# GpSimd adds the whole adjacency mask, TensorE adds none of it, and VectorE makes the mask at the end of its step

## The chip, the cores and the metric
The kernel runs on one core of one Trainium2 chip. The metric is the time of one execution on the device, in microseconds (us), given as the median of several runs. The core has five engines that run their own instruction streams and wait for each other by semaphores: TensorE (PE in the rows; PEld is its weight load), VectorE (DVE), ScalarE (ACT), GpSimd (POOL) and SyncE (SP, which here only issues DMAs). A semaphore wait holds back everything that stands behind it on its engine.

## The reference
One graph attention layer on 4096 nodes, all inputs float32 except the 4096 x 4096 integer adjacency `adj`:

```
h        = relu(layernorm(x))                                   # 4096 x 256
neib_att = tanh(neigh @ Wn1 + bn1) @ Wn2 + bn2                   # 4096 x 32
value    = neigh @ Wv + bv                                       # 4096 x 128
x_att    = tanh(h @ Wx1 + bx1) @ Wx2 + bx2                       # 4096 x 32
ws       = leaky_relu(x_att @ neib_att.T, slope 0.01)            # 4096 x 4096
ws       = where(adj > 0, ws, -9e15); ws = softmax(ws, axis=1)
out      = x + concat([h @ Wfx + bfx, ws @ value], axis=1)       # 4096 x 256
```

## The kernel before
A first phase (to about 47 us) makes `neib_att` and turns `neigh` for `value`. The main phase goes over the 4096 x 4096 scores in **chunks** of 128 rows by 1024 columns, two PSUM banks each: 4 chunks make a tile of 128 rows, 4 tiles a group, 8 groups the matrix, 128 chunks in all. `main` gives every engine the same step counter s, and in step s each engine does its part of several chunks. The order on each engine is written out by hand in its `step` function; nothing else schedules. For chunk s:

- VectorE makes the mask (`mask_of`, L642): 0 where there is an edge, -2^53 where there is none, bf16, 128x1024, from the loaded adjacency. Two mask buffers take turns, four `adj_in` slots are filled two at a time.
- TensorE makes the scores (`score`, L860 and L861) in two halves of 512 columns, in one of two PSUM buffers. Up to chunk 18 (`POOL_MASKS` = 19) an identity matmul L860 first adds the mask to both halves. From chunk 19 on it does so for the first half only.
- ScalarE writes 99 x relu(score) to SBUF (the "rise", L512).
- GpSimd adds the mask to the second half in SBUF (L421), from chunk 19 on.
- VectorE joins PSUM and SBUF into the leaky scores with a running row maximum (the "reduce", L676; a custom instruction over 1024 columns). This is in step s + 1, and its end (`leaked`) gives the PSUM buffer free for the scores of chunk s + 2.
- ScalarE does the exponentials two chunks at a time (L524, 2048 columns), five steps later, so in every odd step.

Nineteen steps behind, the second half of the pipeline turns the exponentials of a whole group (L884, four 128x128 transposes for each of 32 column blocks), splits the result in a high part (`hi`, ScalarE L489) and a low part (`lo`, VectorE L655), and multiplies both with the values (L903, L904, L905). Each step does two blocks, called u = 0 and u = 1. In the steps that are left of a group of 16, the next group's rows are normalised, turned and multiplied (VectorE L546 to L611, GpSimd's Newton steps L375 to L392 and sums L357 and L364), and finished rows are written.

VectorE's order in a step from 19 on is: reduce of chunk s-1, `lo` 0, mask of chunk s+1, `lo` 1, and the small work of the group. TensorE's is: turn 0, scores, product of the last step's block 0, turn 1, product of the last step's block 1, small work. GpSimd's is: add of chunk s, in odd steps the DMA of two adjacency chunks (L400), sums, Newton steps.

Of the kernel before, what the change touches and what calls it, by code (L numbers as in the profile page):

```python
# [27 lines left out]
BF16 = mybir.dt.bfloat16  # L28
INT32 = mybir.dt.int32
ALU = mybir.AluOpType  # L30
# [3 lines left out]
P = 128  # L34
N_X, N_NEIGH, D_IN, D_HID, D_OUT = 4096, 4096, 256, 32, 128
KT = D_IN // P
BANK = 512
GROUP = BANK
TILES = GROUP // P
GROUPS = N_X // GROUP  # L40
NEIGH_GROUPS = N_NEIGH // GROUP
CHUNK = 2 * BANK
CHUNKS = N_NEIGH // CHUNK
STEPS = GROUPS * TILES * CHUNKS
GSTEPS = TILES * CHUNKS
BLOCKS = N_NEIGH // P
PERIOD = 2 * GSTEPS
# [31 lines left out]
X_LEFT_LOAD, X_SUM = 4, 9  # L79
X_RIGHT = 6  # L80
V_START, V_STRIDE = 1, 2
POOL_MASKS = BACK_LAG
WARM_UP = 12
NEWTON = 3
NEWTON_OPS = 2 + 4 * NEWTON
# [2 lines left out]
def build(nc, x, adj, neigh, wx1, bx1, wx2, bx2, wn1, bn1, wn2, bn2, wv, bv, wfx, bfx, out):  # L88
    with ExitStack() as ctx:
        def sb(name, shape, dt):  # L90
            return ctx.enter_context(nc.sbuf_tensor(name, shape, dt))
# [20 lines left out]
        b_fx = sb("b_fx", [P, 1, D_OUT], FP32)  # L112
        ident = sb("ident", [P, P], FP32)
        b_v = sb("b_v", [P, 1, D_OUT], FP32)
        ident_bf16 = sb("ident_bf16", [P, P], BF16)
        top = sb("top", [P, 2, CHUNKS], FP32)
        neg_top = sb("neg_top", [P, 2, 1], FP32)
        sums = sb("sums", [P, 2, TILES, HALVES], FP32)
# [224 lines left out]
        @block.gpsimd  # L343
        def _(pool):
            pool.memset(ident[:, :], 0.0).then_inc(fills, 1)
            pool.memset(ident_bf16[:, :], 0.0).then_inc(fills, 1)
            pool.wait_ge(fills, 2)
            pool.affine_select(out=ident[:, :], in_=ident[:, :], compare_op=ALU.not_equal, fill=1.0,
                               base=0, pattern=[[-1, P]], channel_multiplier=1).then_inc(made, 1)
            pool.affine_select(out=ident_bf16[:, :], in_=ident_bf16[:, :], compare_op=ALU.not_equal, fill=1.0,  # L350
                               base=0, pattern=[[-1, P]], channel_multiplier=1).then_inc(made, 1)

            def left_sum(e, h):
# [59 lines left out]
                right_sum(0, h)  # L413

            def step(s, it):
                if POOL_MASKS <= s < STEPS:

                    parity, tile, c = chunk_of(s)
                    pool.wait_ge(risen, s + 1 + PERIOD * it)
                    half = scores[:, parity * TILES + tile, c * CHUNK + BANK:(c + 1) * CHUNK]  # L420
                    pool.tensor_tensor(half, half, mask[:, s % 2, BANK:CHUNK], ALU.add).then_inc(masked, 1)  # L421
                n = s - LOAD + 1 + ADJ_RING
                if n % LOAD == 0 and ADJ_RING <= n < STEPS:
                    pool.wait_ge(mask_done, s + 1 + PERIOD * it)
                    load_adj(n, n // CHUNKS + 2 * TILES * it)
                for i in range(2):
                    if e := x_due(s, X_SUM + i):
                        left_sum(e + 2 * it, i)
                for i in range(2):
                    if (g := right_due(s - i)) is not None:  # L430
                        right_sum(g + 2 * it, i)
                for i in range(NEWTON + 1):
                    if e := x_due(s, X_RSTD[i]):
                        rstd_of(e + 2 * it, i)
# [104 lines left out]
        def _(dve):  # L539
# [94 lines left out]
            def mask_of(n, it):  # L634

                k = n + PERIOD * it
                dve.wait_ge(adj_ready[n % ADJ_RING // LOAD], 16 * (n // ADJ_RING + 1) + 16 * PERIOD // ADJ_RING * it)
                if n >= 2:
                    dve.wait_ge(scored, k - 1)
                if n - 2 >= POOL_MASKS:  # L640
                    dve.wait_ge(masked, k - 1 - POOL_MASKS)
                dve.tensor_scalar(mask[:, n % 2, :], adj_in[:, n % ADJ_RING, :], 0.0, MASKED, ALU.is_le,  # L642
                                  ALU.mult).then_inc(mask_done, 1)

# [11 lines left out]
                                  ALU.subtract).then_inc(lo_done, 1)  # L656

            def step(s, it):
                if s < POOL_MASKS:
                    mask_of(s + 1, it)  # L660
                n = s - 1
                if 0 <= n < STEPS:

                    parity, tile, c = chunk_of(n)
                    k = n + PERIOD * it
                    cols = scores[:, parity * TILES + tile, c * CHUNK:(c + 1) * CHUNK]
                    dve.wait_ge(risen, k + 1)
                    if n >= POOL_MASKS:
                        dve.wait_ge(masked, k + 1 - POOL_MASKS)
                    if c:  # L670
                        dve.wait_ge(leaked, k)
                    start = top[:, tile % 2, c - 1:c] if c else -3.0e38
                    if c == 0 and n >= 2 * CHUNKS:
                        dve.wait_ge(top_done, n // CHUNKS - 1 + 2 * TILES * it)
                    dve.sem_inc(joined, 1)
                    dve.tensor_tensor_reduce(cols, ps[:, n % 2], cols, SLOPE, start, ALU.add, ALU.max,  # L676
                                             top[:, tile % 2, c:c + 1]).then_inc(leaked, 1)
                lo(s, 0, it)
                if POOL_MASKS <= s < STEPS - 1:
                    mask_of(s + 1, it)  # L680
                if value_due(s - 2) is not None:
                    value_low(value_due(s - 2))
                if s == 1:
                    att_high(1, NEIGH_GROUPS - 1)
                    att_low(1, NEIGH_GROUPS - 1)
                lo(s, 1, it)
                if 0 <= n < STEPS and n % CHUNKS == CHUNKS - 1:
                    dve.wait_ge(leaked, n + 1 + PERIOD * it)
                    if n >= 2 * CHUNKS:

                        dve.wait_ge(exp_done, (n // CHUNKS - 1) * HALVES + 2 * TILES * HALVES * it)
                    dve.tensor_scalar(neg_top[:, n // CHUNKS % 2, :], top[:, n // CHUNKS % 2, CHUNKS - 1:CHUNKS],
                                      -1.0, None, ALU.mult).then_inc(top_done, 1)
# [46 lines left out]
        def _(pe):  # L740
# [91 lines left out]
                if i == TILES - 1:  # L832
                    last.then_inc(x_wide, 1)

            pe.wait_ge(made, 2)
            for _ in range(WARM_UP):
                pe.transpose(pa[:, 1, 0:P], ident[:, :], ident[:, :])
            turn_rows(0, 0, 0)
# [3 lines left out]
            def score(s, h, it):  # L842

                if s >= STEPS:
                    return
                k = s + PERIOD * it
                parity, tile, c = chunk_of(s)
                if h == 0:
                    pe.wait_ge(mask_done, k + 1)
                    if s >= 2:  # L850
                        pe.wait_ge(leaked, k - 1)
                    if s < CHUNKS:

                        pe.wait_ge(att_out, NEIGH_GROUPS - 1 if s == 1 else (s + 1) * CHUNK // GROUP)
                    if tile == 0 and c == 0:
                        pe.wait_ge(x_att, s // GSTEPS + 2 * it + 1)
                half = slice(h * BANK, (h + 1) * BANK)
                on_pool = h == 1 and s >= POOL_MASKS
                if not on_pool:
                    pe.matmul(ps[:, s % 2, half], ident_bf16[:, :], mask[:, s % 2, half], start=True, stop=False)  # L860
                last = pe.matmul(ps[:, s % 2, half], xs[:, parity, tile * P:(tile + 1) * P],  # L861
                                 neib[:, c * CHUNK + h * BANK:c * CHUNK + (h + 1) * BANK], start=on_pool, stop=True)
                if h == 1:
                    last.then_inc(scored, 1)

# [98 lines left out]
```

## Time and profile before

| what | value |
|---|---|
| time, median of 3 runs | 548.64 us (547.9 to 549.05) |
| the profiled execution | 552.71 us, span 550.5 us |
| TensorE busy | 505.3 us, 92% |
| VectorE busy | 478.2 us, 87% |
| ScalarE busy | 432.7 us, 79% |
| GpSimd busy | 211.8 us, 38% |
| mean granted TensorE clock | 0.983 of full speed |

The span is the time from the first to the last instruction of the profiled execution. Busy time is time in which an engine's compute instructions run; the ends of matmuls are modelled and overlap, so the distance from one matmul's start to the next says more than its length. A group of 16 steps repeats itself in the middle of the run with a period of 59.0 us.

### The profile page before, as it was taken

Reading aid. Unit: us, or ns where it says so; the run is one execution under the profiler, and the core shown is the slowest. Engines: PE = TensorE matmul, PEld = TensorE weight load, DVE = VectorE, ACT = ScalarE, POOL = GpSimd, SP = SyncE. Lnnn points to the kernel's source line nnn. Section 1 sums busy time; section 2 is a strip of 40 time slices with the busy share of each in tenths; the row PEclk is TensorE's granted clock in tenths of the full one; section 3 lists DMA queues with packets and bytes.
Section 4 is the critical chain, followed back from the end, with each engine's and each line's share of the span. In section 5 each row is a group of like instructions: output and inputs, shape, how many; then the busy total and the mean of one; then the engine's idle time right before and its main releaser. Section 6 shows DMA issues by size and latency. Waiting matters only on the chain.

```text
span 550.5 us, 8742 instructions
## 1 busy us (share of the span) xinstructions
PE 505.3 (92%) x2759; PEld 378.3 (69%) x2759; DVE 478.2 (87%) x883; ACT 432.7 (79%) x585; POOL 211.8 (38%) x325
## 2 busy tenths in 40 slices
PE   5798788899999999999999999999999999998996
PEld 4455556677777767766877677766777686776784
DVE  2669897999999999999999999999998999996664
ACT  2563688898888888888888878888888889897553
POOL 1402123234633654355434553456435444440100
PEclk8898999899999999999999999999999999999999
DMA  7752865454456545664356445643565445620100
GB/s 205 190 166 48 143 135 98 92 115 78 76 87 139 89 69 96 117 135 76 59 107 147 73 78 113 119 91 64 95 114 96 77 74 94 113 46 1 40 1 19
DMA packets 38013, 52.00 MB, mean 94 GB/s; under 512 B 3920, under 2 KB 29776, under 8 KB 37968
## 3 DMA queue, kind: packets, MB, share of 16 engines
q0 software_dynamic: 9216, 33.56, 37.5%
q1 hardware_dynamic: 28752, 17.90, 11.3%
q8 instruction: 22, 0.36, 0.3%
q14 instruction: 23, 0.19, 0.1%
HBM read 80.81 MB, written 4.19 MB: 154 GB/s over the span
## 4 chain that ended last, share of the span: by engine, by line
PE 34%; DVE 16%; issue 11%; ACT 11%; POOL 7%; DMA 3%; DVEq 1%; POOLq 0%; ACTq 0%
PE ps_turned L884 10%; POOL scores L421 6%; DVE pt_lo L655 5%; PE ps_scores L861 5%; PE ps_product L903 4%; PE ps_product L905 4%; PE ps_product L904 4%; ACT scores L512 4%; ACT scores L524 4%; DVE mask L642 4%; DVE scores L676 3%; PE ps_scores L860 3%; DMA adj_in<-in_adj 3%; ACT pt_hi L489 2%; PE ps_product L814 1%
## 5 line engine op out<-in xcount | busy, mean ns | idle before, releaser
L421 POOL TENSOR_TENSOR scores<-scores,mask 128x512 f32<-128x512 f32 x109 | 129.2, 1186 | 203.6 <-ACT scores L512 203.6
L655 DVE TENSOR_TENSOR pt_lo<-ps_turned,pt_hi 128x512 fp32r<-128x512 f32 x256 | 175.1, 685 | 32.1 <-ACT pt_hi L489 15.9
L489 ACT ACTIVATE pt_hi<-ps_turned 128x512 fp32r<-128x512 f32 x256 | 152.5, 597 | 55.6 <-PE ps_turned L884 49.5
L884 PE MATMUL ps_turned<-ident,scores 128*128 128x128 f32 x1024 | 158.3, 277 | 11.4 <-DVE pt_lo L655 11.0
L884 PEld LDWEIGHTS ps_turned<-ident,scores 128*128 128x128 f32 x1024 | 119.9, 141 | 61.3 <-DVE pt_lo L655 30.4
L512 ACT ACTIVATE scores<-ps_scores 128x1024 f32<-128x1024 f32 x128 | 131.1, 1025 | 28.7 <-PE ps_scores L861 25.9
L524 ACT ACTIVATE scores<-scores,neg_top 128x2048 f32<-128x2048 f32 x64 | 127.9, 1998 | 0.0
L676 DVE CUSTOM_DVE_ANT_0 scores<-ps_scores,scores,top 128x1024 f32<-128x1024 f32 x96 | 122.2, 1273 | 2.8 <-ACT scores L512 0.9
L903 PE MATMUL ps_product<-pt_hi,v_hi 128*128 128x512 f32 x256 | 113.1, 442 | 0.2 <-DVE pt_lo L655 0.2
L861 PE MATMUL ps_scores<-neib,xs 128*128 128x512 f32 x256 | 109.9, 507 | 0.0
L905 PE MATMUL ps_product<-pt_lo,v_hi 128*128 128x512 f32 x256 | 101.4, 396 | 0.0
L904 PE MATMUL ps_product<-pt_hi,v_lo 128*128 128x512 f32 x256 | 100.6, 393 | 0.0
L642 DVE TENSOR_SCALAR mask<-adj_in 128x1024 bf16<-128x1024 bf16 x128 | 87.8, 687 | 5.7 <-DMA adj_in<-in_adj 5.5
L860 PE MATMUL ps_scores<-mask,ident_bf 128*128 128x512 bf16 x147 | 57.2, 389 | 16.5 <-DVE mask L642 10.4
L905 PEld LDWEIGHTS ps_product<-pt_lo,v_hi 128*128 128x128 f32 x256 | 48.0, 188 | 11.1
L861 PEld LDWEIGHTS ps_scores<-neib,xs 128*128 128x128 f32 x256 | 49.9, 195 | 3.8
L903 PEld LDWEIGHTS ps_product<-pt_hi,v_hi 128*128 128x128 f32 x256 | 48.4, 189 | 5.4 <-DVE pt_lo L655 0.7
L904 PEld LDWEIGHTS ps_product<-pt_hi,v_lo 128*128 128x128 f32 x256 | 48.7, 190 | 4.6
L400 POOL DMA_DIRECT2D adj_in<-in_adj x64 | 36.9, 577 | 32.5 <-DVE mask L642 32.4
L676 DVE CUSTOM_DVE_ANT_0 scores<-ps_scores,scores 128x1024 f32<-128x1024 f32 x32 | 39.0, 1219 | 4.5 <-issue 2.0
L860 PEld LDWEIGHTS ps_scores<-mask,ident_bf 128*128 128x128 bf16 x147 | 14.3, 97 | 31.5 <-DVE mask L642 18.9
L830 PEld LDWEIGHTS ps_product<-w_fx,x_rows_t 128*128 128x128 f32 x128 | 19.8, 199 | 2.6
(76 smaller groups left out, 385.1 us busy)
## 6 DMA issues: line engine op xcount, KB each, us to landing
adj_in<-in_adj POOLq DMA_DIRECT2D x64, 512.0 KB, 5.5
scores<-in_L_gnn_neigh SPq DMA_DIRECT2D x8, 512.0 KB, 4.3
x_rows<-in_x SPq DMA_DIRECT2D x8, 512.0 KB, 6.6
x_left<-in_x SPq DMA_DIRECT2D x8, 256.0 KB, 5.7
x_right<-in_x SPq DMA_DIRECT2D x8, 256.0 KB, 2.9
out_h<-x_left SPq DMA_DIRECT2D x8, 256.0 KB, 2.3
out_h<-x_right SPq DMA_DIRECT2D x8, 256.0 KB, 5.1
scores<-in_x SPq DMA_DIRECT2D x1, 512.0 KB, 5.0
```

The source lines that it names most:

```text
L421: pool.tensor_tensor(half, half, mask[:, s % 2, BANK:CHUNK], ALU.add).then_inc(masked, 1)
L489: act.activation(pt_hi[:, (2 * b + u) % HI_RING], pt[:, u], ACT.Copy).then_inc(hi_done, 1)
L512: act.activation(scores[:, parity * TILES + tile, c * CHUNK:(c + 1) * CHUNK], ps[:, s % 2], ACT.Relu, scale=RISE).then_inc(risen, 1)
L524: act.activation(cols, cols, ACT.Exp, bias=neg_top[:, tile % 2, :], accum_out=sums[:, parity, tile, c // 2:c // 2 + 1]).then_inc(exp_done, 1)
L642: dve.tensor_scalar(mask[:, n % 2, :], adj_in[:, n % ADJ_RING, :], 0.0, MASKED, ALU.is_le, ALU.mult).then_inc(mask_done, 1)
L655: dve.tensor_tensor(pt_lo[:, u], pt[:, u], pt_hi[:, (2 * b + u) % HI_RING].bitcast(FP32), ALU.subtract).then_inc(lo_done, 1)
L676: dve.tensor_tensor_reduce(cols, ps[:, n % 2], cols, SLOPE, start, ALU.add, ALU.max, top[:, tile % 2, c:c + 1]).then_inc(leaked, 1)
L861: last = pe.matmul(ps[:, s % 2, half], xs[:, parity, tile * P:(tile + 1) * P], neib[:, c * CHUNK + h * BANK:c * CHUNK + (h + 1) * BANK], s ...
L884: last = pe.transpose(pt[:, u, i * P:(i + 1) * P], scores[:, parity * TILES + i, n * P:(n + 1) * P], ident[:, :])
L903: pe.matmul(acc, v_hi[:, n, :], pt_hi[:, b2_ % HI_RING, :], start=n == 0, stop=False)
L904: pe.matmul(acc, v_lo[:, n, :], pt_hi[:, b2_ % HI_RING, :], start=False, stop=False)
L905: pe.matmul(acc, v_hi[:, n, :], pt_lo[:, b2_ % 2, :], start=False, stop=n == BLOCKS - 1).then_inc(block_used, 1)
```

## The change
GpSimd now adds the mask of every chunk, both halves, in two instructions of 128x512, in every step from 0 on; before each pair it waits for the rise and for the mask. TensorE's identity matmuls and the bf16 identity are gone, and `score` no longer waits for the mask. In VectorE's step the mask of the next chunk is made after `lo` 1 in all steps; before, it was made between the two `lo` from step 19 on, and ahead of the reduce in the steps up to 18. The reduce waits for both halves' adds (`masked`, now two per chunk) instead of the rise.

```
-POOL_MASKS = BACK_LAG
...
 def step(s, it):                      # GpSimd
-    if POOL_MASKS <= s < STEPS:
+    if s < STEPS:
         parity, tile, c = chunk_of(s)
-        pool.wait_ge(risen, s + 1 + PERIOD * it)
-        half = scores[:, parity * TILES + tile, c * CHUNK + BANK:(c + 1) * CHUNK]
-        pool.tensor_tensor(half, half, mask[:, s % 2, BANK:CHUNK], ALU.add).then_inc(masked, 1)
+        pool.wait_ge(risen, s + 1)
+        pool.wait_ge(mask_done, s + 1)
+        for h in range(2):
+            half = scores[:, parity * TILES + tile, c * CHUNK + h * BANK:c * CHUNK + (h + 1) * BANK]
+            pool.tensor_tensor(half, half, mask[:, s % 2, h * BANK:(h + 1) * BANK], ALU.add).then_inc(
+                masked, 1)
...
 def mask_of(n, it):                   # VectorE
     if n >= 2:
-        dve.wait_ge(scored, k - 1)
-    if n - 2 >= POOL_MASKS:
-        dve.wait_ge(masked, k - 1 - POOL_MASKS)
+        dve.wait_ge(masked, 2 * (k - 1))
...
 def step(s, it):                      # VectorE
-    if s < POOL_MASKS:
-        mask_of(s + 1, it)
...
-        dve.wait_ge(risen, k + 1)
-        if n >= POOL_MASKS:
-            dve.wait_ge(masked, k + 1 - POOL_MASKS)
+        dve.wait_ge(masked, 2 * (k + 1))
...
     lo(s, 0, it)
-    if POOL_MASKS <= s < STEPS - 1:
-        mask_of(s + 1, it)
...
     lo(s, 1, it)
+    if s < STEPS - 1:
+        mask_of(s + 1, it)
...
 def score(s, h, it):                  # TensorE
     if h == 0:
-        pe.wait_ge(mask_done, k + 1)
...
-    on_pool = h == 1 and s >= POOL_MASKS
-    if not on_pool:
-        pe.matmul(ps[:, s % 2, half], ident_bf16[:, :], mask[:, s % 2, half], start=True, stop=False)
     last = pe.matmul(ps[:, s % 2, half], xs[:, parity, tile * P:(tile + 1) * P],
-                     neib[:, ...], start=on_pool, stop=True)
+                     neib[:, ...], start=True, stop=True)
```

GpSimd, steps 76 to 78 (the middle of the main phase): before, two steps stand merged in the first row, then the DMA, six Newton steps and the next add.

```order
184 L421 TENSOR_TENSOR scores<-scores,mask 128x512 [waits risen] x2
185 L400 DMA adj_in<-in_adj 128x2048 [waits mask_done]
186 L375 TENSOR_SCALAR var_eps<-mean_var 128x4 [waits newton,aggr_done,x_normed]
187 L379 TENSOR_SCALAR rstd<-var_eps 128x4 [waits newton]
188 L385 TENSOR_TENSOR factor<-rstd 128x4 [waits newton]
189 L387 TENSOR_TENSOR factor<-factor,var_eps 128x4 [waits newton]
190 L390 TENSOR_SCALAR factor<-factor 128x4 [waits newton]
191 L392 TENSOR_TENSOR rstd<-rstd,factor 128x4 [waits newton]
192 L421 TENSOR_TENSOR scores<-scores,mask 128x512 [waits risen]
```

The same place of the changed kernel:

```order
304 L418 TENSOR_TENSOR scores<-scores,mask 128x512 [waits mask_done,risen]
305 L418 TENSOR_TENSOR scores<-scores,mask 128x512
306 L418 TENSOR_TENSOR scores<-scores,mask 128x512 [waits mask_done,risen]
307 L418 TENSOR_TENSOR scores<-scores,mask 128x512
308 L395 DMA adj_in<-in_adj 128x2048 [waits mask_done]
309 L370 TENSOR_SCALAR var_eps<-mean_var 128x4 [waits newton,aggr_done,x_normed]
...
314 L387 TENSOR_TENSOR rstd<-rstd,factor 128x4 [waits newton]
315 L418 TENSOR_TENSOR scores<-scores,mask 128x512 [waits mask_done,risen]
316 L418 TENSOR_TENSOR scores<-scores,mask 128x512
```

Each step has two adds back to back, and the DMA and the Newton steps stand behind both.

VectorE, step 77, from the reduce of chunk 76 to that of chunk 77, before:

```order
486 L676 ISA scores,top<-ps_scores,scores 128x1024 [waits top_done,risen,masked]
487 L676 ISA top 128x1
488 L655 TENSOR_TENSOR pt_lo<-ps_turned,pt_hi 128x512 [waits block_used,hi_done]
489 L642 TENSOR_SCALAR mask<-adj_in 128x1024 [waits masked,scored,adj_ready1]
490 L655 TENSOR_TENSOR pt_lo<-ps_turned,pt_hi 128x512 [waits block_used,hi_done]
491 L554 BN_AGGR mean_var<-stats 128x2 [waits newton,stats_done,x_normed]
492 L554 BN_AGGR mean_var<-stats 128x2 x3
493 L600 TENSOR_SCALAR xs<-ps_product,b 128x512 [waits scored,x_second]
494 L676 ISA scores,top<-ps_scores,scores,top 128x1024 [waits leaked,risen,masked]
```

And in the changed kernel:

```order
428 L668 ISA scores,top<-ps_scores,scores 128x1024 [waits masked,top_done]
429 L668 ISA top 128x1
430 L651 TENSOR_TENSOR pt_lo<-ps_turned,pt_hi 128x512 [waits block_used,hi_done] x2
431 L638 TENSOR_SCALAR mask<-adj_in 128x1024 [waits masked,adj_ready1]
432 L552 BN_AGGR mean_var<-stats 128x2 [waits newton,stats_done,x_normed]
433 L552 BN_AGGR mean_var<-stats 128x2 x3
434 L598 TENSOR_SCALAR xs<-ps_product,b 128x512 [waits scored,x_second]
435 L668 ISA scores,top<-ps_scores,scores,top 128x1024 [waits masked,leaked]
```

The mask now stands behind both `lo` and ahead of the group's small work, which stands between it and the next reduce.

## Rows read from the trace of the kernel before

**Rows 1.** Busy time in stretches of 18, 107 and 16 steps, each from one reduce's start.

```profile
core 0: us, PE busy (x) PEld busy (x) DVE busy (x) ACT busy (x) POOL busy (x), PEclk, DMA share, GB/s
51.21:100.57 49.36, 41.30 (x248) 29.83 (x246) 42.56 (x87) 37.27 (x43) 9.85 (x25) 0.97 0.66 118
104.52:494.90 390.38, 373.17 (x2059) 282.66 (x2057) 370.07 (x680) 338.28 (x455) 186.03 (x253) 1.00 0.52 95
273.49:332.51 59.02, 56.53 (x313) 42.81 (x313) 56.33 (x107) 50.74 (x70) 29.11 (x42) 1.00 0.53 99
```

**Rows 2.** Page, groups of instructions: busy us, mean ns, idle before and releaser.

```profile
L421 POOL TENSOR_TENSOR scores<-scores,mask 128x512 f32<-128x512 f32 x109 | 129.2, 1186 | 203.6 <-ACT scores L512 203.6
...
L642 DVE TENSOR_SCALAR mask<-adj_in 128x1024 bf16<-128x1024 bf16 x128 | 87.8, 687 | 5.7 <-DMA adj_in<-in_adj 5.5
L860 PE MATMUL ps_scores<-mask,ident_bf 128*128 128x512 bf16 x147 | 57.2, 389 | 16.5 <-DVE mask L642 10.4
...
L400 POOL DMA_DIRECT2D adj_in<-in_adj x64 | 36.9, 577 | 32.5 <-DVE mask L642 32.4
```

**Rows 3.** VectorE's masks in one period, 273.49 to 332.51 us.

```profile
L642 DVE TENSOR_SCALAR mask<-adj_in 128x1024 bf16<-128x1024 bf16 x16 | 11.7, 729 | 0.3 <-DMA adj_in<-in_adj 0.3
```

**Rows 4.** Timeline, steps 76 to 79: start, us, engine, line.

```profile
311.81 0.42 DVE L642 TENSOR_SCALAR mask<-adj_in 128x1024 bf16<-128x1024 bf16 x1
...
312.41 0.66 PE L884 MATMUL ps_turned<-ident,scores 128*128 128x128 f32 x4
...
312.90 0.38 PE L860 MATMUL ps_scores<-mask,ident_bf 128*128 128x512 bf16 x1
...
313.57 0.39 PE L903 MATMUL ps_product<-pt_hi,v_hi 128*128 128x512 f32 x1
...
314.91 0.60 ACT L489 ACTIVATE pt_hi<-ps_turned 128x512 fp32r<-128x512 f32 x1
...
315.40 1.99 ACT L524 ACTIVATE scores<-scores,neg_top 128x2048 f32<-128x2048 f32 x1
...
317.76 1.27 DVE L676 CUSTOM_DVE_ANT_0 scores<-ps_scores,scores,top 128x1024 f32<-128x1024 f32 x1
...
317.86 1.02 ACT L512 ACTIVATE scores<-ps_scores 128x1024 f32<-128x1024 f32 x1
...
318.96 0.68 DVE L655 TENSOR_TENSOR pt_lo<-ps_turned,pt_hi 128x512 fp32r<-128x512 f32 x1
...
322.07 1.28 DVE L676 CUSTOM_DVE_ANT_0 scores<-ps_scores,scores,top 128x1024 f32<-128x1024 f32 x1
```

**Rows 5.** Timeline, a mask and GpSimd's two instructions around it.

```profile
245.04 1.16 POOL L421 TENSOR_TENSOR scores<-scores,mask 128x512 f32<-128x512 f32 x1 [1.65 <-ACT scores L512]
...
245.22 1.26 DVE L642 TENSOR_SCALAR mask<-adj_in 128x1024 bf16<-128x1024 bf16 x1
...
246.16 0.91 POOL L357 TENSOR_TENSOR x_left<-x_left,b_fx 128x256 f32<-128x256 f32 x1
```

**Rows 6.** Timeline, an add and the reduce that waits for it.

```profile
493.56 1.16 POOL L421 TENSOR_TENSOR scores<-scores,mask 128x512 f32<-128x512 f32 x1 [2.92 <-ACT scores L512]
...
494.90 1.28 DVE L676 CUSTOM_DVE_ANT_0 scores<-ps_scores,scores,top 128x1024 f32<-128x1024 f32 x1 [0.20 <-POOL scores L421]
```

**Rows 7.** Timeline, steps 2 to 5 and GpSimd's Newton steps of steps 13 to 15.

```profile
56.40 1.27 DVE L676 CUSTOM_DVE_ANT_0 scores<-ps_scores,scores,top 128x1024 f32<-128x1024 f32 x1
...
60.73 1.27 DVE L676 CUSTOM_DVE_ANT_0 scores<-ps_scores,scores,top 128x1024 f32<-128x1024 f32 x1
...
62.16 0.38 PE L860 MATMUL ps_scores<-mask,ident_bf 128*128 128x512 bf16 x1 [0.62 <-DVE top L676]
...
86.62 0.22 POOL L375 TENSOR_SCALAR var_eps<-mean_var 128x4 f32<-128x4 f32 x1 [4.84 <-DVE mean_var L554]
...
91.80 0.38 POOL L392 TENSOR_TENSOR rstd<-rstd,factor 128x4 f32<-128x4 f32 x1
```

More of the change, by code:

```diff
@@ L114, in build @@
         b_v = sb("b_v", [P, 1, D_OUT], FP32)
-        ident_bf16 = sb("ident_bf16", [P, P], BF16)
         top = sb("top", [P, 2, CHUNKS], FP32)
@@ L345, in _ @@
             pool.memset(ident[:, :], 0.0).then_inc(fills, 1)
-            pool.memset(ident_bf16[:, :], 0.0).then_inc(fills, 1)
-            pool.wait_ge(fills, 2)
+            pool.wait_ge(fills, 1)
             pool.affine_select(out=ident[:, :], in_=ident[:, :], compare_op=ALU.not_equal, fill=1.0,
-                               base=0, pattern=[[-1, P]], channel_multiplier=1).then_inc(made, 1)
-            pool.affine_select(out=ident_bf16[:, :], in_=ident_bf16[:, :], compare_op=ALU.not_equal, fill=1.0,
                                base=0, pattern=[[-1, P]], channel_multiplier=1).then_inc(made, 1)
@@ L833, in x_wide_layer @@
                     last.then_inc(x_wide, 1)
-            pe.wait_ge(made, 2)
+            pe.wait_ge(made, 1)
             for _ in range(WARM_UP):
@@ L857, in score @@
                 half = slice(h * BANK, (h + 1) * BANK)
-                on_pool = h == 1 and s >= POOL_MASKS
-                if not on_pool:
-                    pe.matmul(ps[:, s % 2, half], ident_bf16[:, :], mask[:, s % 2, half], start=True, stop=False)
                 last = pe.matmul(ps[:, s % 2, half], xs[:, parity, tile * P:(tile + 1) * P],
-                                 neib[:, c * CHUNK + h * BANK:c * CHUNK + (h + 1) * BANK], start=on_pool, stop=True)
+                                 neib[:, c * CHUNK + h * BANK:c * CHUNK + (h + 1) * BANK], start=True, stop=True)
                 if h == 1:
```

## Prediction, made before the changed kernel ran
> **What bounds the kernel now.** I read the windows of the main phase first, then the groups of the page, then the timeline of a few steps. The windows [rows 1] are cut at starts of the reduce L676: 18 steps take 49.36 us at the start (2.74 a step), the next 107 take 390.38 us (3.65 a step), and one period of 16 takes 59.02 us (3.69 a step). In that period VectorE is busy 56.33 us and TensorE 56.53; the reader is to see two engines near full, ScalarE 8 us below, and GpSimd at half. Part of VectorE's busy time is a stall: a mask takes 0.42 us when GpSimd is idle [rows 4], but 0.69 on average [rows 2] and 0.73 in the period [rows 3]. In [rows 5] a mask started at 245.22 while GpSimd's add ran to 246.20; the mask ended at 246.48, so it stood until the add was over and then did its work in 0.28 us. GpSimd's next instruction had begun at 246.16 and was itself held until the mask was through. So such a mask pays for the rest of the running add, and gets in between two GpSimd instructions.
> The Trainium skill, "SBUF — State Buffer", section "SBUF: two separate sides", says that VectorE in its two-port modes and GpSimd share a port pair as an exclusive lock, and that the loser blocks fully. The trace agrees (0.42 against 1.26 us), and the rule speaks against a change that doubles GpSimd's adds. It does not say who is next after two adds back to back; [rows 5] does, once.
>
> **The change part by part.**
> TensorE loses the identity matmuls, 147 of them [rows 2]. The price of one is not its modelled 389 ns but what it holds up the order: from L860 to L903 three matmuls take 0.67 us [rows 4], so 0.22 each. Scores are also no longer kept waiting by the mask (page: 16.5 us idle before L860, 10.4 by the mask). If TensorE alone set the pace that would be 147 x 0.22 = 32 us; with the wait to the mask some more.
> GpSimd gets 147 more adds. One is 1.16 to 1.19 us [rows 2, 6]; a pair 2.31, since the second begins 0.05 before the first ends, as in [rows 5]. The skill's "GPSIMD Engine Reference", section 3.1, gives 4497 ns for such an add of 2048 elements, a quarter of which is 1.12 us; the row is used. With half a DMA issue a step (0.58 / 2 [rows 2]) and 0.28 for a mask that gets in, GpSimd needs 2.9 us a step, under 3.65 but over 2.74.
> The move of the mask on VectorE adds no instruction. But the reduce waits for both adds, and the group's small work now stands behind the mask.
>
> First the middle (steps 19 to 126). Let R(n) be the start of the reduce of chunk n.
> VectorE's own work a step, each instruction counted to the start of the next: reduce 1.20, two `lo` 0.60 each, mask 0.34 unstalled: 2.74 [rows 4]. Small work: 56.33 busy less 16 x 1.20, 32 x 0.60 and 11.7 - 16 x 0.08 of masks leaves 7.5 us a period, 0.47 a step [rows 1, 3]. Together 3.2 a step: VectorE could run at 51 us a period if nothing kept it.
> Chain A: reduce n (1.20), `lo` 0 (0.68), turn 0 of the next step (0.49 to the scores), both score matmuls until ScalarE can start (0.62), rise (1.02), the pair of adds (2.31), reduce n+2. That is 6.32 us and five handoffs of 0.05 to 0.18 ([rows 6]: add's end 494.72, reduce 494.90), 0.35 together: 6.67 for two steps.
> Chain B, over the exponentials in odd steps: from the turn at 312.41 over `hi` 1 and the exponential (314.91, 315.40) to the end of the next rise at 318.88 are 6.47 us [rows 4], without the identity matmul 6.25. Before it stand reduce and `lo` of an odd chunk (1.94 with the handoff), behind it the pair and two handoffs (2.56). So R(odd n) to R(n+3) is at least 10.75.
> With w the interval to an odd chunk's reduce and y that to an even one's: w + y >= 6.67, w + 2y >= 10.75, and w >= 2.74 + 0.47 = 3.2. To each pair comes 0.1 to 0.28 for the mask that gets in or follows; with 0.2, y = (10.95 - 3.2) / 2 = 3.88, and w + y = 7.08, or 56.6 us a period against 59.02. So far the change gains: before, one such interval was 4.31 [rows 4].
> Two things eat this. First, GpSimd's other work now stands behind a pair. The Newton steps ran from 86.62 to 92.2 in three steps, and the sums are four of 0.75 (0.91 in [rows 5], held). The next pair can be ready 0.9 to 1.3 us after the reduce; 1.8 us of Newton work, or 1.1 and a DMA issue of 0.58, or two sums, comes too late. I get delays of 0.9, 0.2, 0.7 and 0.3, about 2 us a period. Second, when a mask is asked for in the second half of the pair it ends 0.28 after the pair, and the small work (0.3 to 1.0 us) then stands bare ahead of the reduce; in the present order much of it runs beside the add. The mask is asked for 2.4 us after the reduce; I laid out the 16 steps of a period with these prices, and this happens in seven of them, 0.3 to 0.65 us each less what has slack, about 2 us. The intervals came out as 3.4, 4.0, 3.45, 4.2, 3.35, 3.7, 3.1, 4.8, 3.1, 4.0, 3.8, 4.2, 3.75, 4.0, 3.55 and 4.2, together 60.6 us: 1.6 more than before. Over 107 steps, 6.7 periods, +11; the last periods have less small work, so I take +9.
>
> Then the start (steps 0 to 18), where GpSimd did no add. Here chain C closes over the two PSUM buffers: reduce n to scores of n+2 is 1.43 (60.73 to 62.16 [rows 7]), scores 0.66, rise 1.02, pair 2.31, two handoffs 0.25: 5.67 for two steps, with the mask between the halves 5.95, or 2.98 a step. GpSimd's own 2.9 is close under it, so its Newton steps (4.3 us of work in the 5.6 of [rows 7]) and sums (1.4) are paid in part; I take 3 of the 5.7. The reduce of chunk 0 waits 1.5 longer, and that of chunk 1, before at 56.40 [rows 7], comes at 57.9; 17 steps of 2.98 and 3 more end at 111.6, against 100.57. Some of this may be given back, since before, a mask waited there for its DMA (5.5 us in all [rows 2]) and that wait is now covered: +9 at the start. The adjacency load is issued after the pair now, with 5.5 us to landing; the mask that needs it comes some 7 us later, so it is hidden, by little.
> The last 50 us have no scores and no mask: nothing.
> Sum: the profiled execution is 552.71, its span 550.5 and 2.2 around it; plus 18 is 570.7. The median of the runs is 548.64, 4.1 below the profiled one, so I forecast 566.6, rounded to 566.
>
> **The bounds of what no row shows.** Two adds back to back, with a mask asking in between: at best a pair is 2.31 and the mask waits for nothing (GpSimd's side then 0.2 a step cheaper: -25), at worst each pair and mask are 2.31 + 0.42 + handoff with the small work bare each time (0.47 x 125 = 59, of which what hides under ScalarE's chain B is at least two thirds: +20 at most). I stand nearer to [rows 5], which is the same meeting once: the price of 0.28. The first scores start earlier by the mask's 0.4 us or by nothing; nothing taken.
>
> **The rivals.**
> (1) Faster: the mask's stall goes. In the period masks cost 11.7 us, 16 x 0.42 would be 6.7; if the mask always falls where VectorE would wait anyway, and TensorE gives back 0.22 a step, the middle takes the 56.6 us period of the bare chains: -2.4 x 6.7 = -16. With a start that costs only +6 (chain C without meetings, 2.84 a step, and GpSimd's other work hidden) the time is 539. For it: VectorE and TensorE are the two full engines [rows 1] and both lose work. Against: chain C is 0.1 over the present pace even at its best. It decides where GpSimd's Newton steps and sums do not reach the next pair.
> (2) No change: gain in the middle (-9) and loss at the start (+9) cancel; 549.
> (3) Much slower: GpSimd's pair is not parted, and the mask waits for the second half whenever it comes during the pair. Then about seven further steps of each period show their small work bare, at 0.26 net each: 7 x 0.26 x 6.7 = 12 more, 578. The skill's words in the section named, that the loser waits for the whole instruction, leave this open. Against it is [rows 5].
> (4) TensorE's clock: in the start it is granted 0.97 [rows 1] with TensorE busy 41.30 of 49.36 us; with the identity matmuls gone and longer waits it could fall in part of the start. At half the clock for 20 us, where it is busy half the time and the chain holds 1.1 us of it in 5.95, that is +4, 570; within my own case's range.
>
> **How the numbers follow.** My case (560 to 573): 0.60. Rival 3 and beyond: 0.17. Rival 1: 0.11. Between it and my case lies 549 to 560 with rival 2: 0.12. What a measurement can tell from no change is about 0.2%, 1.1 us. Faster 0.13, same 0.03, slower 0.84. The range from 552 to 580 leaves out rivals 1 and 2 and the far end of 3.
>
> **What would show it.** In the profile after: GpSimd busy near 384 us (211.8 of the page and 147 x 1.17); the pair 2.31, or 2.6 with a mask in it; 18 steps of the start near 58 us; a period near 60.6; VectorE's busy share lower with idle time before the reduce, released by GpSimd's add; TensorE idle before its turn, released by `lo`. A period under 58 would show that the queue behind the pair does not matter; masks with durations over 1.5 us would show rival 3. A start under 52 us would break chain C.

## The result and the profile after

| what | before | after |
|---|---|---|
| time, median | 548.85 us | 573.98 us (571.1 to 575.11, 4 runs) |
| ratio of the runs | 1 | 1.0435, 95% interval 1.0369 to 1.0501 |
| profiled execution, its span | 552.71, 550.5 | 574.46, 572.3 |
| GpSimd busy | 211.8 us | 380.3 us |
| TensorE, VectorE, ScalarE busy | 505.3, 478.2, 432.7 | 485.1, 477.3, 432.9 |

The change costs 25 us by the medians, 24 by the ratio, 21.8 between the two profiled spans; forecast were 17 to 18. The windows of the changed kernel, cut at starts of the reduce (now L668) of the same chunks as in [rows 1]: start (reduce 0 to 18), middle (19 to 126), one period (64 to 80). Columns as in [rows 1].

```profile
core 0: us, PE busy (x) PEld busy (x) DVE busy (x) ACT busy (x) POOL busy (x), PEclk, DMA share, GB/s
52.08:115.25 63.17, 42.85 (x218) 32.60 (x217) 51.73 (x88) 39.59 (x46) 51.37 (x62) 0.89 0.51 92
118.72:516.85 398.13, 353.90 (x1962) 268.20 (x1961) 360.05 (x680) 337.69 (x454) 309.66 (x361) 1.00 0.50 93
288.07:348.59 60.52, 53.38 (x298) 40.33 (x297) 54.47 (x105) 50.74 (x69) 47.24 (x58) 1.00 0.51 96
```

The start takes 13.8 us longer for 18 steps, the middle 7.8 for 107. So two thirds of the loss lie in a tenth of the run. The reader is to see that no engine is as near to full as before: in the period TensorE fell from 56.5 to 53.4 us (96% to 88%) and VectorE from 56.3 to 54.5 (95% to 90%), while the period grew by 1.5.

Groups of the page of the changed kernel, to be held against [rows 2]:

```profile
L418 POOL TENSOR_TENSOR scores<-scores,mask 128x512 f32<-128x512 f32 x256 | 299.5, 1190 | 96.8 <-ACT scores L510 96.4
...
L872 PE MATMUL ps_turned<-ident,scores 128*128 128x128 f32 x1024 | 160.2, 279 | 49.4 <-DVE pt_lo L651 48.1
...
L638 DVE TENSOR_SCALAR mask<-adj_in 128x1024 bf16<-128x1024 bf16 x128 | 87.4, 683 | 3.5 <-DMA adj_in<-in_adj 3.3
L668 DVE CUSTOM_DVE_ANT_0 scores<-ps_scores,scores 128x1024 f32<-128x1024 f32 x32 | 39.1, 1222 | 26.7 <-POOL scores L418 26.7
```

An add costs what it cost (1190 against 1186 ns), there are 147 more. The reduce, which the page of before showed waiting hardly at all for GpSimd, waits for it; for the 32 chunks at the head of a tile these are 26.7 us, for the 96 others 11.1. And TensorE idles 49.4 us ahead of its turns, 48.1 of them for VectorE's `lo`, which stands behind that reduce. This is the chain A of the prediction.

The timeline of the changed kernel over steps 76 to 78, the place of [rows 4]:

```profile
330.67 4.72 POOL L418 TENSOR_TENSOR scores<-scores,mask 128x512 f32<-128x512 f32 x4 [1.05 <-ACT scores L510]
...
331.71 0.42 DVE L638 TENSOR_SCALAR mask<-adj_in 128x1024 bf16<-128x1024 bf16 x1
...
333.37 1.22 DVE L668 CUSTOM_DVE_ANT_0 scores<-ps_scores,scores 128x1024 f32<-128x1024 f32 x1 [0.84 <-POOL scores L418]
...
336.97 1.27 DVE L668 CUSTOM_DVE_ANT_0 scores<-ps_scores,scores,top 128x1024 f32<-128x1024 f32 x1
...
338.43 2.47 POOL L418 TENSOR_TENSOR scores<-scores,mask 128x512 f32<-128x512 f32 x2
...
339.37 0.50 DVE L638 TENSOR_SCALAR mask<-adj_in 128x1024 bf16<-128x1024 bf16 x1
...
341.12 1.28 DVE L668 CUSTOM_DVE_ANT_0 scores<-ps_scores,scores,top 128x1024 f32<-128x1024 f32 x1 [0.45 <-POOL scores L418]
```

The pair at 330.67 is followed at once by the next chunk's (four adds in 4.72 us). The mask at 339.37 falls in a pair: it takes 0.50 and the pair 2.47 instead of some 2.3, so it did get in between the two adds, as [rows 5] had it. Over the whole trace 39 of the 128 masks started during the first add of a pair: 37 of them ended 1.4 to 1.5 us after the pair's start, having got in between the two adds, and two (at 73.32 and 85.16) only 2.6 us after it. The 68 that started during a second add ended 2.55 to 2.7 us after the pair's start. The reduce of chunk 78 waits 0.45 us for the end of its pair. The interval from reduce 76 to 77 is 3.60, to 78 another 4.15.

### The profile page after: what moved, and what is told of

Same layout as the page of the kernel before. It is cut to its first block, busy times and chain, and to the rows that moved or that the text cites. A ratio compares the mean times of both kernels' runs of the same rounds, so it can differ in the third digit from the quotient of the medians.

```text
span 572.3 us, 8493 instructions
## 1 busy us (share of the span) xinstructions
PE 485.1 (85%) x2612; PEld 364.6 (64%) x2612; DVE 477.3 (83%) x883; ACT 432.9 (76%) x585; POOL 380.3 (66%) x470
## 3 DMA queue, kind: packets, MB, share of 16 engines
q1 hardware_dynamic: 28752, 17.90, 10.4%
## 4 chain that ended last, share of the span: by engine, by line
PE 48%; DVE 25%; issue 13%; POOL 5%; ACT 4%; DMA 1%; DVEq 1%; POOLq 0%; SPq 0%; ACTq 0%
PE ps_turned L872 16%; DVE pt_lo L651 10%; PE ps_product L893 7%; PE ps_product L891 7%; PE ps_product L892 7%; PE ps_scores L849 6%; DVE scores L668 4%; POOL scores L418 4%; DVE mask L638 3%; DVE x_rows L592 2%; ACT scores L510 2%; ACT scores L522 1%; DMA scores<-in_L_gnn_neigh 1%; PE ps_product L759 1%; DVE top L668 1%
## 5 line engine op out<-in xcount | busy, mean ns | idle before, releaser
L418 POOL TENSOR_TENSOR scores<-scores,mask 128x512 f32<-128x512 f32 x256 | 299.5, 1190 | 96.8 <-ACT scores L510 96.4
L872 PE MATMUL ps_turned<-ident,scores 128*128 128x128 f32 x1024 | 160.2, 279 | 49.4 <-DVE pt_lo L651 48.1
L651 DVE TENSOR_TENSOR pt_lo<-ps_turned,pt_hi 128x512 fp32r<-128x512 f32 x256 | 168.4, 685 | 25.5 <-PE ps_product L893 16.6
L668 DVE CUSTOM_DVE_ANT_0 scores<-ps_scores,scores,top 128x1024 f32<-128x1024 f32 x96 | 122.5, 1276 | 11.2 <-POOL scores L418 11.1
L849 PE MATMUL ps_scores<-neib,xs 128*128 128x512 f32 x256 | 93.0, 445 | 20.1 <-DVE top L668 18.2
L668 DVE CUSTOM_DVE_ANT_0 scores<-ps_scores,scores 128x1024 f32<-128x1024 f32 x32 | 39.1, 1222 | 26.7 <-POOL scores L418 26.7
L893 PEld LDWEIGHTS ps_product<-pt_lo,v_hi 128*128 128x128 f32 x256 | 48.2, 188 | 11.2
L849 PEld LDWEIGHTS ps_scores<-neib,xs 128*128 128x128 f32 x256 | 39.8, 196 | 24.0 <-DVE top L668 21.4
L359 POOL TENSOR_TENSOR x_right<-x_right,b_v 128x256 f32<-128x256 f32 x16 | 12.3, 776 | 22.9 <-DMA x_right<-in_x 22.8
L822 PEld LDWEIGHTS ps_product<-w_fx,x_rows_t 128*128 128x128 f32 x128 | 21.2, 215 | 3.5 <-DVE xs L603 0.8
L352 POOL TENSOR_TENSOR x_left<-x_left,b_fx 128x256 f32<-128x256 f32 x16 | 12.8, 800 | 15.6 <-DMA x_left<-in_x 15.5
```

The costliest lines, as they stand in the source:

```text
L418: pool.tensor_tensor(half, half, mask[:, s % 2, h * BANK:(h + 1) * BANK], ALU.add).then_inc(masked, 1)
L651: dve.tensor_tensor(pt_lo[:, u], pt[:, u], pt_hi[:, (2 * b + u) % HI_RING].bitcast(FP32), ALU.subtract).then_inc(lo_done, 1)
L872: last = pe.transpose(pt[:, u, i * P:(i + 1) * P], scores[:, parity * TILES + i, n * P:(n + 1) * P], ident[:, :])
L893: pe.matmul(acc, v_hi[:, n, :], pt_lo[:, b2_ % 2, :], start=False, stop=n == BLOCKS - 1).then_inc(block_used, 1)
```

## The experiments

All times are medians; the ratio is that of the runs' means to the kernel before on the same chip, whose median was 552.56 us beside e1 to e4, 549.27 beside e5 to e8 and 548.83 beside e9 to e12. "Start" and "middle" are the distances in us between the reduces of chunks 0 and 18, and of 19 and 126, in each kernel's one trace; "clock" is the granted clock of TensorE in the start.

| kernel | us | ratio (95%) | start | middle | clock |
|---|---|---|---|---|---|
| before | 548.85 | 1 | 49.4 | 390.4 | 0.97 |
| after | 573.98 | 1.0435 (1.0369 to 1.0501) | 63.2 | 398.1 | 0.89 |
| e1 middle only | 557.39 | 1.011 (1.0033 to 1.0186) | 51.4 | 398.1 | 0.93 |
| e2 start only | 567.25 | 1.030 (1.0221 to 1.0379) | 65.0 | 392.4 | 0.84 |
| e3 mask in its old places | 593.01 | 1.0749 (1.0679 to 1.0819) | 73.7 | 408.9 | 0.82 |
| e4 short queue | 564.45 | 1.0263 (1.0181 to 1.0346) | 59.8 | 394.4 | 0.94 |
| e5 scores twice | 573.99 | 1.0418 (1.0331 to 1.0506) | 65.8 | 400.5 | 0.95 |
| e6 two masks | 560.27 | 1.0176 (1.0111 to 1.0242) | 60.1 | 387.5 | 0.87 |
| e7 mask last | 567.7 | 1.0304 (1.0239 to 1.037) | 62.9 | 396.2 | 0.86 |
| e8 no identity | 540.37 | 0.9804 (0.9734 to 0.9874) | 51.4 | 381.5 | 0.93 |
| e9 one add | 571.61 | 1.0421 (1.0363 to 1.0479) | 62.1 | 399.8 | 0.89 |
| e10 half masked | 536.3 | 0.9778 (0.9722 to 0.9834) | 53.5 | 371.6 | 0.90 |
| e11 odd pairs | 556.84 | 1.0143 (1.0099 to 1.0187) | 51.3 | 394.6 | 0.93 |
| e12 odd pairs, mask at end | 559.28 | 1.0198 (1.0145 to 1.025) | 49.4 | 395.8 | 0.99 |

e1, e8, e11 and e12 have the start of the kernel before, word for word, and it came out between 49.4 and 51.4 us; so a start is known to 2 us. The same holds of a middle: e2 has that of the kernel before (392.4 against 390.4), e1 and e5 that of the changed kernel (398.1 and 400.5 against 398.1). Differences of 2 us in either stretch say nothing by themselves. The first phase also varies by 5.7 us between the traces (the reduce of chunk 0 begins at 46.6 to 52.3), which is why the stretches say more than the medians.

The 2 us of the start go with the clock. Of the five starts with the same code, the two at 0.97 and 0.99 took 49.4 us (before, e12) and the three at 0.93 took 51.3 to 51.4 (e1, e8, e11); e11 and e12 ran on the same chip. The difference arises in the first nine steps, and in the first six of these the clock of e1, e8 and e11 was about 0.8. The start of the changed kernel took 63.2 us at 0.89 and, in e2, 65.0 at 0.84. No run sets the clock by itself, so this is a correlation.

**e1, the middle alone; e2, the start alone.**

```
e1:  POOL adds: 2 halves if s >= 19 else 0;   mask: "end" if s >= 19 else ahead of the reduce
e2:  POOL adds: 1 half  if s >= 19 else 2;    mask: "between the lo" if s >= 19 else "end"
```

> Only the middle changed: chunks 0 to 18 are masked by TensorE as before, with the mask ahead of the reduce; from chunk 19 on GpSimd adds both halves and the mask is made at the end of the step. Theory (start and middle lose by mechanisms of their own, 13.8 and 7.8 us in the traces): 549 + 8 = 557, start 49.4 us for 18 steps, period 60.5. Rival (the middle loses only because the start leaves the engines in another phase): 549 to 551, period 59.

> Only the start changed: GpSimd adds both halves of chunks 0 to 18 with the mask at the step's end; from 19 on all is as before. Theory: 549 + 14 = 563, 18 steps in 63 us, period 59.0. Rival (the phase in which the start ends matters for the middle): the period is not 59.0 and the sum of the two parts alone misses 25 us by more than 4.

In the stretches both came out as the theory has it: the middle costs 7.7 us in the one trace (398.1 against 390.4), the start 15.7 in the other, and the ratios 1.011 and 1.030 add up to 1.041 where the whole is 1.0435. But both signs of e2's rival can be read off too: the period of chunks 64 to 80 is 60.7 us in e2, not 59.0, and by the medians the parts add up to 4.8 and 14.7, or 19.5, which misses 25 by 5.6. The period first: it is one of six to seven in the middle, and that of e1 is 59.9 where the changed kernel has 60.5 with the same code. The whole middle of e2 is 2.0 us longer than that of the kernel before, and two equal middles differ by 2.4 elsewhere. So start and middle are two losses, and what the one does to the other is at most about 2 us.

**e3, the mask in its old places.**

```
-                lo(s, 1, it)
-                if s < STEPS - 1:
-                    mask_of(s + 1, it)
+                (ahead of the reduce for s < 19, between lo 0 and lo 1 from 19 on)
```

> The changed kernel with the mask in its old places (ahead of the reduce up to step 18, between the two lo from 19 on). Theory (the pair of adds is what costs; the place decides only what of the small work stands bare and how often a mask meets a pair): 568 to 573, a little faster than the changed kernel, masks longer in the middle, less small work bare. Rival (the move of the mask is the loss): under 560.

Both theories failed. I had held the move for nearly neutral; it is worth 17 us to the changed kernel by the ratios (in the traces 10.5 in the start and 10.7 in the middle). The trace of e3 shows two waits in the start:

```profile
77.63 0.71 POOL L411 DMA_DIRECT2D adj_in<-in_adj  x1
...
78.81 2.27 POOL L434 TENSOR_TENSOR scores<-scores,mask 128x512 f32<-128x512 f32 x2 [0.46 <-ACT scores L526]
...
83.19 0.72 DVE L656 TENSOR_SCALAR mask<-adj_in 128x1024 bf16<-128x1024 bf16 x1 [3.57 <-DMA adj_in<-in_adj]
...
83.83 1.21 DVE L691 CUSTOM_DVE_ANT_0 scores<-ps_scores,scores 128x1024 f32<-128x1024 f32 x1
...
105.69 0.43 DVE L656 TENSOR_SCALAR mask<-adj_in 128x1024 bf16<-128x1024 bf16 x1 [1.62 <-POOL scores L434]
...
106.15 1.28 DVE L691 CUSTOM_DVE_ANT_0 scores<-ps_scores,scores,top 128x1024 f32<-128x1024 f32 x1
```

The first is the larger. The adjacency load of the mask is issued by GpSimd at 77.63, behind a pair, and the mask starts at 83.19, 5.6 us later, when the load has landed. The adds of the chunk that the reduce at 83.83 needs ended at 81.08: the reduce stood 2.7 us behind a mask that it did not need. Masks of e3's start wait 14.9 us for loads, in five waits, against 2.0 in the changed kernel's, where the mask is asked for later. The second wait is for the mask buffer. There are two, and the mask of chunk s+1 goes into that of chunk s-1. It must wait for the end of that chunk's adds (7.9 us in the start), the same event that the reduce waits for, and standing ahead of the reduce it is put into the chain: 0.46 us from its start to the reduce's. In the middle the mask between the two `lo` is held by a running add for longer (914 ns on average between 200 and 450 us of the trace against 649), and `lo` 1, for which TensorE waits, stands behind it; VectorE is busy 389 of the 409 us there, against 360 of 398.

**e4, a short queue on GpSimd.** It leaves out the Newton refinement of the reciprocal root and, from the second group on, the adding of the two biases.

```
-NEWTON = 3
+NEWTON = 0
...
 def left_sum(e, h):
     pool.wait_ge(x_left_in, 16 * (e + 1))
+    if e: pool.sem_inc(x_summed, 1); return
```

> The changed kernel with GpSimd's other work cut: no Newton refinement of the reciprocal root (only its two first instructions) and, from the second group on, no sums of the biases; the waits and signals stay. Theory (what stands behind the pair on GpSimd delays the next pair by some 2 us a period, and by some 3 us in the start): period near 58.5, time 574 - 13 - 3 = 558. Rival (the chain of rise, pair and reduce alone sets the period): period 60.2 or more, time 570 or more.

In between: 3.7 us of the middle and 3.4 of the start go, where 13 and 3 were expected. The work behind the pair costs, but in the middle little over a quarter of what I had put on it. In the start the clock differs too (0.94 against 0.89), so not all of the 3.4 need be the queue.

**e5, the scores twice in the start.**

```
-                last = pe.matmul(ps[:, s % 2, half], ...)
+                for _ in range(2 if s < BACK_LAG else 1):
+                    last = pe.matmul(ps[:, s % 2, half], ...)
```

> The changed kernel with the score matmuls of chunks 0 to 18 made twice into the same place, which gives TensorE back the busy time that the identity matmuls had there. Theory (part of the start's loss is TensorE's clock, granted 0.89 there against 0.97 before): clock back to 0.95 or more, the start no longer than 63 us although 0.44 us stand more in the chain of two steps (+4 us by themselves). Rival (the clock costs nothing there): start 67 us, time 578.

The granted clock of the start rose from 0.89 to 0.95. The start is 2.6 us longer, between the two theories' numbers; with the expected 4 us added by the matmuls themselves the clock would be worth 1.4 us, or 3.2 against the 65.0 of e2. Neither settles it alone. The starts of equal code in the table say more: about 2 us for 0.04 to 0.05 of clock. At that rate the fall from 0.97 to 0.89 is worth some 3 us of the 13.8, an estimate.

**e6, two masks.** VectorE computes the masks of chunks 0 and 1 only; GpSimd adds stale ones for the rest.

```
+                if n >= 2:
+                    dve.sem_inc(mask_done, 1)
+                    return
```

> The changed kernel in which VectorE makes only the masks of chunks 0 and 1; for all others it waits and signals as before but computes nothing, so the adds use stale masks. No mask meets an add any more. Theory (the chains of rise, pair, reduce hold the pace; the meetings cost 0.2 per pair of steps): period 58.5 to 59.5, start 59, time 560. Rival (the meetings of masks and adds are the main loss): at or under 549.

The time is as expected (560.27), the period 58.1 a little under it: middle 10.7 and start 3.0 us shorter than in the changed kernel. Even with no masks made, so none to meet an add, the kernel is slower than before, now by its start alone (60.1 against 49.4). The windows of its start and middle:

```profile
52.31:112.44 60.13, 42.65 (x215) 32.30 (x214) 38.27 (x70) 39.22 (x45) 49.77 (x61) 0.87 0.53 94
115.49:502.95 387.46, 351.65 (x1961) 268.60 (x1960) 304.55 (x572) 337.10 (x453) 302.54 (x361) 1.00 0.53 96
```

VectorE is 79% busy in this middle and the pace hardly better than that of the kernel before (387.5 us against 390.4): the chain holds it, not VectorE's work.

**e7, the mask as the last of VectorE's step.**

```
-                if s < STEPS - 1:
-                    mask_of(s + 1, it)            # behind lo 1
...
+                if s < STEPS - 1:
+                    mask_of(s + 1, it)            # behind the small work of the group
```

> The changed kernel with the mask behind the group's small work, as the very last of VectorE's step. Theory (small work behind a mask that waits for the pair stands bare ahead of the reduce, 2 us a period): period 58.5 to 59.5, time 561 to 567. Rival (a mask asked for later meets the pair's second half more often and the next pair must wait for it): 574 or more.

567.7, at the edge of what was expected. The direction is right (ratio 1.0304 against 1.0435, the period 59.5 against 60.5), but in the whole middle it is 2.0 us, no more than equal middles differ by. Of the 6.4 us between the two profiled spans 4.1 lie ahead of the first reduce, in the first phase that the edit does not touch. So the bare small work is a small term, and these runs can't tell it from nothing.

**e8, TensorE's share alone.** The kernel before without the identity matmul from chunk 19 on: the first half of these chunks is not masked.

```
-                if not on_pool:
+                if not on_pool and s < POOL_MASKS:
```

> The kernel before, in which TensorE leaves out the identity matmul from chunk 19 on (the first half of each of these chunks is not masked); nothing else is changed, and TensorE still waits for the mask. It prices what the change takes from TensorE, by itself. Theory (VectorE's order with its stalls sets the pace, TensorE's 0.22 us a step is cover): 545 to 549 and a period of 58 or more. Rival (TensorE sets the pace): 549 - 24 = 525, period 55.5.

The middle is 8.9 us shorter (to about 2 us), 0.083 a step of the 0.22 that a matmul holds up TensorE's order. More than my theory, far less than the rival's 24: TensorE is part of the chains but does not set the pace alone.

**e9, one add of 128x1024.**

```
-                    for h in range(2): ... pool.tensor_tensor(half, half, mask[...], ALU.add).then_inc(masked, 1)
+                    pool.tensor_tensor(whole, whole, mask[:, s % 2, :], ALU.add).then_inc(masked, 2)
```

> The changed kernel with one add of 128x1024 in place of the pair, so that no mask can get in between the halves. Theory (a mask gets in between the two instructions, which costs 0.28 at most; when it can't, it waits up to 2.3 us and the small work behind it stands bare, 12 us as in rival 3 of the prediction): masks up to 2.5 us long, period 61.5 to 62.5, time 580 to 588. Rival (parted or not is the same, and one instruction saves one start): 570 to 575.

The time is that of the changed kernel, so the rival's 570 to 575 came and not the theory's 580 to 588. The timeline of e9:

```profile
310.80 2.14 POOL L417 TENSOR_TENSOR scores<-scores,mask 128x1024 f32<-128x1024 f32 x1 [1.91 <-ACT scores L508]
...
311.78 1.44 DVE L636 TENSOR_SCALAR mask<-adj_in 128x1024 bf16<-128x1024 bf16 x1
...
313.21 1.21 DVE L666 CUSTOM_DVE_ANT_0 scores<-ps_scores,scores 128x1024 f32<-128x1024 f32 x1
```

The mechanism of rival 3 is there: the mask waits until 312.94 for the whole add, and masks take 937 ns on average instead of 683. But in this place the mask ends when the reduce may start anyway, and the one add is 2.14 us, 0.17 less than a pair. Price: none to be seen.

**e10, only half of each mask.** The changed kernel in which GpSimd adds the second half only; the first half of every chunk is not masked.

```
-                    for h in range(2):
+                    for h in range(1, 2):
```

> The changed kernel in which GpSimd adds only the second half of each chunk's mask (the first half of every chunk stays unmasked). It takes 1.15 us out of each chain and leaves all else. Theory (the second add is the loss): start 63.2 - 9 x 1.15 - 3 = 50 us for 18 steps, period 57.0 to 58.0, middle 384, time about 546. Rival (something else in the new order costs, such as the mask's place): start over 55, period over 59, time over 555.

```profile
46.86:100.39 53.53, 38.95 (x212) 29.32 (x211) 44.96 (x88) 37.97 (x45) 30.09 (x43) 0.90 0.60 106
103.77:475.35 371.58, 350.35 (x1958) 268.31 (x1957) 347.63 (x680) 332.30 (x454) 186.61 (x253) 0.99 0.55 100
```

The second add is the loss: 9.6 us of the start, where 13.2 were expected, and 26.6 of the middle, where 14 were. In the middle the rest of the change is a gain (371.6 against 390.4 us), though 8.9 of it e8 has too, by leaving half of the scores unmasked; in the start it is not (53.5 against 49.4).

**e11 and e12, can part of it be had?** From chunk 19 on, GpSimd adds both halves of odd chunks only, TensorE keeps its identity matmul for even ones. e11 keeps the masks where they were; e12 makes the mask of odd chunks behind the second `lo`.

```
+def on_pool(s): return (1 + s % 2) if s >= BACK_LAG else 0
e12: mask: "end" if s % 2 == 0 else "between the lo", for s >= 19
```

> The kernel before, in which from chunk 19 on the odd chunks have both halves added by GpSimd and lose their identity matmul; even chunks, whose rise stands behind the exponential, stay as they were. Masks in their old places. Theory (an odd chunk's reduce came 2.0 to 3.0 us after its rise anyway, so a pair of 2.31 and its handoffs fit there nearly free, and TensorE gives back 0.22 in every second step): period 58.2 to 58.8, time 0 to 4 us under before. Rival (masks between the two lo meet the pair's longer run): slower than before, period over 59.3.

> As the kernel with odd pairs, and in even steps the mask (that of the next, odd chunk, which TensorE does not wait for) is made behind the second lo. Theory: lo 1 of the even steps no longer stands behind a stalled mask; period 57.5 to 58.5, time 2 to 6 us under before. Rival (the mask meets the add there as often): no better than the kernel with odd pairs and masks in the old places.

Both are slower than before, by 1.4% and 2%, and the middle is 4.2 and 5.4 us longer (2.2 and 3.4 against e2's). The time and period (59.6) of e11 are the rival's, its reason is not: a mask takes 779 ns there between 200 and 450 us of the trace, but 760 in the kernel before, so the masks are held hardly longer than they were. In e12 it is 685, and the middle is no better. What grew in both middles are two waits of VectorE: reduces wait 11.0 and 11.2 us for GpSimd (0.7 before), and masks 6.2 and 9.2 us for the adjacency load (1.1 before), which GpSimd issues. That these waits are the loss was not tested. No kernel that computes the reference beat the kernel before.

## Why the prediction was right, and where its steps were not

The direction and the mechanism hold: e10 takes the second add out and the loss of the middle is gone, with most of the start's. e8 and e10 split the +7.7 of the middle (the three parts add up by construction, each is known to about 2 us): from before to e8 the identity matmuls go (-8.9); from e8 to e10 the mask moves to the end and TensorE no longer waits for it (-9.9); from e10 to the changed kernel comes the second add (+26.6). e3, which undoes only the move in the changed kernel, gives a term of the second's size from the other side (+10.7).

- **The period.** 60.6 was forecast, 60.52 came. That it fits to 0.1 is luck: the same middle code gave 59.9 in e1 and 60.6 in e5, and that of the kernel before 59.0 and, in e2, 60.7. Over the whole middle 16 steps take 59.5 us against 58.4 before, +1.2 and not +1.6. Its intervals from chunk 64 on are 3.33, 3.94, 3.49, 4.11, 3.21, 3.85, 2.88, 4.75, 4.16, 3.53, 3.58, 4.47, 3.60, 4.15, 3.33, 4.14, within 0.3 of the list of the prediction but for the ninth (4.16 for 3.1) and the tenth (3.53 for 4.0). But the two terms that I laid over the bare chains were both too large: GpSimd's queue, "about 2 us a period", cost 3.7 in the whole middle (e4), and the bare small work, also 2 a period, cost 2.0 in the whole middle (e7), within the noise. So the bare chains at 56.6 us a period were too short; e6, with no meeting of mask and add at all, still has a period of 58.1. Even without its 0.2 for the meeting the prediction's chains give 55.8, and e4 leaves only some 0.6 a period to the queue. The sum was right by errors of both signs.
- **The middle as a whole.** +9 taken, +7.75 measured.
- **The start.** Chain C holds (e10: one add less is 9.6 us, where nine turns of the chain less 1.15 each are 10.4), but +9 was too little against 13.8 (14.7 with the reduce of chunk 0, 0.9 later). The working itself ended at 111.6 against 100.57, or +11; I took 2 off for DMA waits that would be covered. That was wrong in kind: the 111.6 had been laid out from the chain alone, with no DMA wait in it to be covered. Of the missing 3.7 us the reduce of chunk 1 has 1.1: it came at 58.96 where 57.9 was expected, and the timeline of the changed kernel shows an instruction that I had not priced.

```profile
55.72 2.44 POOL L418 TENSOR_TENSOR scores<-scores,mask 128x512 f32<-128x512 f32 x2 [3.96 <-ACT scores L510]
...
55.90 2.42 DVE L592 TENSOR_SCALAR x_rows<-x_rows,mean_var,rstd 128x256 f32<-128x256 f32 x2
...
58.96 1.27 DVE L668 CUSTOM_DVE_ANT_0 scores<-ps_scores,scores,top 128x1024 f32<-128x1024 f32 x1
```

  Two normalising instructions take 2.42 us beside a pair of adds. In the trace of the kernel before, at the same place, the two take 0.74:

```profile
54.69 0.74 DVE L594 TENSOR_SCALAR x_rows<-x_rows,mean_var,rstd 128x256 f32<-128x256 f32 x2
```

  So they are held by GpSimd like the masks, and the next two (1.66 us, at 64.65) again. The other 2.6 us came in the 17 steps from chunk 1 to 18, 56.3 where 53.7 was laid out. Besides those two, the granted clock of 0.89 can explain them: rival 4 put 4 us on it, and the starts of equal code make it some 3, an estimate that no run tests by itself.
- **The move of the mask.** The prediction counted it as nothing but a risk to the small work. It was the part of the change that gained most (e3: 10.5 us in the start and 10.7 in the middle; e8 to e10: up to 9.9, together with the wait taken from `score`).
- **Rival 1 (faster)** needed the queue behind the pair to be free. e4 shortened that queue and still lost 2.6%: the second add decides (e10), not what stands behind it. Rival 2 needed a gain of 9 us in the middle, which lost 7.7.
- **Rival 3** has its mechanism in e9, without its price. Its sign, masks over 1.5 us, showed in the changed kernel in two of 128 (1.69 and 2.04 us), both in the start.

## What to carry to other kernels

Before work goes to an idle engine, ask what waits for it: GpSimd had over half its time free, but each added microsecond stood between the rise and the reduce, in a chain that closes every two steps. A part that is taken off a full engine is worth only what lies in such a chain (0.08 of 0.22 us here). Where a buffer ring of two is refilled, the refill waits for the same event as the consumer and for its own load besides; put it behind the consumer, not ahead (10.5 us of the start in e3).

## What the runs showed of the hardware that I had not expected

- One GpSimd add of 128x1024 takes 2142 ns, two of 128x512 in a row 2.28 us.
- Not only the bf16 mask but also VectorE's float32 `tensor_scalar` of 128x256 is held by a running GpSimd add (2.42 us for two, where the same two take 0.74 in the kernel before).
- A mask that waits so for the first of two GpSimd adds back to back got in between them in 37 of 39 cases in the changed kernel (pair 2.47 us, mask 0.50 at 339.37); in two it waited for both. Beside a single long add it waits to the end (mask 1.44 us).
- In equal code, a granted clock of 0.93 in place of 0.97 to 0.99 went with a start of 51.3 to 51.4 us in place of 49.4.
